# Expert weights turned one at a time and 64-row keys in a block of two expert layers around an attention

## The chip, the cores and the metric

The kernel runs on one core of one Trainium2 chip. The metric is the device time of one execution in microseconds, lower is better. The engines are named as the profile names them: PE (matrix), PEld (its weight loads), DVE (vector), ACT (scalar), POOL (GpSimd), SP (the queue that issues most transfers).

## What is computed

The reference, cut to what matters. The input is 16 sequences of 256 tokens with 128 features, 4096 tokens in all.

```python
x = x + 0.5 * ffn(layernorm(x))      # expert layer 0
x = x + attention(layernorm(x))
x = x + 0.5 * ffn(layernorm(x))      # expert layer 1

def ffn(x):                           # 8 experts, each takes its own 512 best tokens
    scores = softmax(xf @ gate_w.T)
    vals, idx = top_k(scores.T, 512)
    y = layernorm(xf[idx]) * ln_w + ln_b
    h = gelu(y @ fc1s[e].T + b1s[e])              # 128 -> 512
    out = (h @ fc2s[e].T + b2s[e]) * vals         # 512 -> 128
    return xf.at[idx].add(out)

def attention(x):                     # 16 heads of 8 features, causal, 256 tokens
    scores = (q @ k.T + q . pek[distance]) / sqrt(8)
    p = softmax(where(causal, scores, -inf))
    return (p @ v + p . pev[distance]) @ Wo.T
```

## The kernel before, in words

Each engine has its own program, and semaphores set the order between them. There are three parts: `expert_layer(0)`, `attention()`, `expert_layer(1)`.

**Expert layer.** DVE normalises the tokens and finds each expert's 512 tokens with a search of 30 steps. Then the token numbers of the experts come out one expert after another. POOL fetches the tokens: `gather(e)` issues four indirect transfers (L543). It issues the gathers of `AHEAD = 5` experts first, then `scatter(0)`: four indirect transfers that add the results into the output in memory (L554). `scatter(e)` waits until the results of expert e are scaled (`s_os`) and until all transfers of `scatter(e - 1)` have landed (`s_sc`), since both may add to the same row. After each scatter comes the gather of expert e + 5, as long as there is one. In layer 0 the later scatters have two memsets each behind them (L570, L571), which clear a quarter of the key buffer of the attention.

PE turns all weights first: 16 banks of four transposes (L913) through two PSUM banks, which ACT copies out (L700, L702). Then, expert by expert: `turn_rows(e)` turns the fetched tokens (L920), DVE scales them into `yT` (`rows_in`, L1308), `first_half(e)` multiplies with fc1 (L929), ACT takes the gelu (L710), and `second_half(e)` multiplies with fc2 (L939). DVE adds the bias and scales (`scale`, L1293, L1296). PE's order is `first_half(e)`, `turn_rows(e + 1)`, `second_half(e - 1)`, so the first result comes after two first halves. ACT also writes `parity` rows for the attention after each expert of layer 0 (L718).

**Projections.** `attention()` projects queries and keys in 16 pieces (L973). Each piece is split into three bf16 parts whose sum is the fp32 value: `first_part` (ACT, L726), `rest_of` (DVE, L1334), `second_part` (ACT, L730), `third_part` (POOL, L591, and L594 for the odd queries). SP stores each piece to memory (L440). From the fifth piece on, one of the nine loads of the first pair of sequences follows each store (L447). `stacked` lists these loads: six products of query and key parts, times 8 features, make 48 rows of a stack in SBUF; the queries have a second 48 rows. The runs hold 3, 2 and 1 products. A query load of a run repeats one part (a broadcast over the run), so its outermost count is the run's length. `first_part(i)` waits for the store of piece i - 4. PE waits for all nine loads before the first scores.

**Scores.** Eight pairs of sequences with 12 slots each. In a slot, `scores` has two halves u. A half is 16 matmuls with the relative keys (L1002, 128 rows) and 16 with the stacked keys (L1005, 128 rows, of which rows 48 and up hold zeros). Between the halves PE turns the maxima that DVE found in the slot before (`turn_maxima`, L1017). After both halves comes `subtract_maxima` of slot s - 2 (L1025), then a `chunk` of the outputs (L1056 or L1066; the first pair has none before its ninth slot). ACT takes the exponential of slot s - 2 (L778) when the subtraction is done. There are three score buffers of two banks, so `scores(s + 1)` waits for the exponential of slot s - 2. On DVE a slot is `partial_maxima` (L1366, L1368) and `rows_of_maxima` (L1382 to L1385), and in four of 12 slots `reduce_relative` (L1395, L1400).

## Time and profile before

| | us or share |
|---|---|
| median of 3 runs (967.27 to 972.53) | 968.02 |
| the profiled execution | 967.66 |
| its span | 965.9 |
| PE busy | 636.5 |
| DVE busy | 504.7 |
| ACT busy | 297.2 |
| POOL busy | 235.6 |
| share of the chain that ended last: PE | 38% |
| DVE, POOL, ACT | 15%, 14%, 9% |
| SP's queue and DMA | 6% and 5% |

Between the span and the execution's time lie 1.76 us. The stretches of the span: expert layer 0 up to about 228 us, the projections up to about 312 us, the scores up to about 712 us, the output projection and expert layer 1 to the end. A row of a timeline gives start, duration, engine, line, operation, what it writes and reads, the count of merged instructions, and in brackets how long the engine was idle before and what ended that. Starts of PE rows can be subtracted from each other; the durations overlap, since matmuls are pipelined.

### The profile page before, as it was taken

Reading aid. Unit: us, or ns where it says so; the run is one execution under the profiler, and the core shown is the slowest. Engines: PE = TensorE matmul, PEld = TensorE weight load, DVE = VectorE, ACT = ScalarE, POOL = GpSimd, SP = SyncE. Lnnn points to the kernel's source line nnn. Section 1 sums busy time; section 2 is a strip of 40 time slices with the busy share of each in tenths; the row PEclk is TensorE's granted clock in tenths of the full one; section 3 lists DMA queues with packets and bytes.
Section 4 is the critical chain, followed back from the end, with each engine's and each line's share of the span. In section 5 each row is a group of like instructions: output and inputs, shape, how many; then the busy total and the mean of one; then the engine's idle time right before and its main releaser. Section 6 shows DMA issues by size and latency. Waiting matters only on the chain.

```text
span 965.9 us, 29195 instructions
## 1 busy us (share of the span) xinstructions
PE 636.5 (66%) x12366; PEld 516.7 (53%) x12366; DVE 504.7 (52%) x1712; ACT 297.2 (31%) x473; POOL 235.6 (24%) x227
## 2 busy tenths in 40 slices
PE   4512998700733789888898879899972811689640
PEld 3501556500422678777787768788862800357430
DVE  7977222123721567565666557667766777512120
ACT  2390454300522232323232313232332264063210
POOL 2000738884533000000000000014110000346864
PEclk9999999955885599999898979999985555599985
DMA  4272213325355332323222323234342506112322
GB/s 122 59 218 80 53 17 43 34 24 142 132 160 173 92 62 70 59 69 60 69 44 74 52 70 56 65 72 97 75 110 46 175 1 178 24 35 31 45 25 22
DMA packets 99163, 73.27 MB, mean 76 GB/s; under 512 B 26569, under 2 KB 92258, under 8 KB 98914
## 3 DMA queue, kind: packets, MB, share of 16 engines
q1 hardware_dynamic: 85858, 57.01, 23.4%
q0 software_dynamic: 13184, 14.43, 9.2%
q8 instruction: 102, 1.67, 0.8%
q14 instruction: 19, 0.16, 0.1%
HBM read 44.34 MB, written 27.01 MB: 74 GB/s over the span
## 4 chain that ended last, share of the span: by engine, by line
PE 38%; DVE 15%; POOL 14%; issue 11%; ACT 9%; SPq 6%; DMA 5%; DVEq 0%; ACTq 0%; POOLq 0%
PE banks L1002 10%; ACT arena L778 8%; PE banks L1005 7%; POOL x_mid L554 5%; PE banks L1025 5%; POOL out_dram L554 5%; SPq L469 3%; DVE arena L1119 3%; PE banks L1066 2%; PE banks L849 2%; POOL arena L543 2%; PE banks L929 2%; PE banks L913 1%; DMA out_dram<-arena 1%; SPq L440 1%
## 5 line engine op out<-in xcount | busy, mean ns | idle before, releaser
L778 ACT ACTIVATE arena<-banks 128x1024 f32<-128x1024 f32 x96 | 98.3, 1024 | 263.4 <-PE banks L1025 263.4
L1002 PE MATMUL banks<-arena 128*128 128x32 bf16 x3072 | 126.8, 194 | 42.8 <-issue 16.1
L1002 PEld LDWEIGHTS banks<-arena 128*128 128x128 bf16 x3072 | 112.4, 101 | 68.1 <-ACT arena L778 38.7
L1366 DVE TRANSPOSE_TENSOR_REDUCE arena<-banks 128x32 f32<-128x1024 f32 x96 | 120.0, 1250 | 18.1 <-PE banks L1005 13.8
L1005 PE MATMUL banks<-arena 128*128 128x32 bf16 x3072 | 108.6, 178 | 8.6 <-issue 8.6
L1005 PEld LDWEIGHTS banks<-arena 128*128 128x128 bf16 x3072 | 93.6, 97 | 11.3 <-issue 11.3
L543 POOL DMA_INDIRECT arena<-table,arena x64 | 61.5, 961 | 126.2 <-DVE arena L1276 107.7
L607 POOL COPY arena<-arena 128x576 f32 (+1 forms) x8 | 5.3, 668 | 329.6 <-PE banks L1056 329.6
L1382 DVE TENSOR_REDUCE arena<-banks 32x8 f32<-32x64 f32 (+1 forms) x96 | 20.1, 209 | 107.9 <-PE banks L1017 107.8
L710 ACT ACTIVATE arena<-banks,arena 128x512 f32<-128x512 f32 x64 | 44.0, 687 | 85.2 <-PE banks L929 85.2
L1025 PE MATMUL banks<-arena 128*128 128x64 bf16 x1536 | 64.4, 198 | 0.7 <-issue 0.7
L929 PE MATMUL banks<-arena 128*128 128x512 f32 x128 | 61.0, 609 | 3.6 <-DVE arena L1308 3.6
L939 PE MATMUL banks<-arena 128*128 128x128 f32 x512 | 61.8, 281 | 1.6 <-ACT arena L710 1.6
L939 PEld LDWEIGHTS banks<-arena 128*128 128x128 f32 x512 | 60.6, 198 | 3.2 <-ACT arena L710 3.2
L554 POOL DMA_INDIRECT out_dram<-arena x32 | 50.2, 1568 | 33.6 <-DVE arena L1296 15.1
L871 PE MATMUL banks<-arena 128*128 128x1 bf16 x60 | 11.2, 186 | 71.4 <-DVE arena L1228 71.4
L1066 PE MATMUL banks<-arena 128*32 128x128 f32 x1536 | 56.4, 288 | 1.4 <-issue 1.2
L554 POOL DMA_INDIRECT x_mid<-arena x32 | 50.2, 1570 | 24.2 <-DVE arena L1296 14.8
L1025 PEld LDWEIGHTS banks<-arena 128*128 128x128 bf16 x1536 | 54.5, 101 | 1.0 <-issue 1.0
L1056 PE MATMUL banks<-arena 128*9 128x128 f32 x1536 | 52.4, 278 | 3.5 <-ACT arena L785 1.9
L1293 DVE TENSOR_TENSOR arena<-banks,arena 128x512 f32<-128x512 f32 x16 | 11.1, 692 | 82.0 <-DMA x_mid<-arena 33.6
L1308 DVE TENSOR_SCALAR arena<-banks,arena 128x512 f32<-128x512 f32 x16 | 13.0, 810 | 73.1 <-PE banks L920 73.1
(182 smaller groups left out, 1021.4 us busy)
## 6 DMA issues: line engine op xcount, KB each, us to landing
query_parts<-arena SPq DMA_DIRECT2D x8, 768.0 KB, 6.4
arena<-query_parts SPq DMA_DIRECT2D x16, 384.0 KB
table<-arena SPq DMA_DIRECT2D x2, 2176.0 KB, 9.4
arena<-in_L_ffn_fc2s_dram SPq DMA_DIRECT2D x4, 1024.0 KB, 10.8
arena<-query_parts SPq DMA_DIRECT2D x16, 256.0 KB
key_parts<-arena SPq DMA_DIRECT2D x8, 384.0 KB, 7.0
arena<-key_parts SPq DMA_DIRECT2D x8, 384.0 KB
head_outputs<-arena SPq DMA_DIRECT2D x128, 18.0 KB
```

The source lines that it names most:

```text
L543: pool.indirect_dma_start(out=rows[:, s, :], out_offset=None, in_=table[n], in_offset=bass.IndirectOffsetOnAxis(ap=idx[:, s:s + 1], axis=0 ...
L554: pool.indirect_dma_start(out=total[n], out_offset=bass.IndirectOffsetOnAxis(ap=idx[:, s:s + 1], axis=0), in_=osb[:, e % 2, j, :], in_offs ...
L710: nc.scalar.activation(hT[:, e % 2, c, :], psum[:, H_B[k % 2], :], ACT.Gelu_apprx_tanh, bias=b1T[:, e * NC + c:e * NC + c + 1]).then_inc(s ...
L778: nc.scalar.activation(dst, psum[:, 2 * r:2 * r + 2, :].rearrange("p u (h n) -> p u h n", h=H), ACT.Exp, scale=HD ** -0.5).then_inc(s_prob, 1)
L929: pe.matmul(psum[:, H_B[k % 2], :], w1T[:, e, P * c:P * c + P], yT[:, e % 2, :], start=True, stop=True).then_inc(s_h, 1)
L939: last = pe.matmul(o, hT[:, e % 2, c, P * j:P * j + P], w2T[:, e, c, :], start=(c == 0), stop=(c == NC - 1))
L1002: pe.matmul(sc[:, :, 2 * a:2 * a + 2], rel_k[:, y:y + P], q_st[:, r, :, q0 + 2 * a:q0 + 2 * a + 2], start=(a == 0), stop=False, skip_group ...
L1005: last = pe.matmul(sc[:, h], k_st[:, r, h, L * b + P * kb:L * b + P * kb + P], q_st[:, r, h, q0:q0 + 32], start=False, stop=False, skip_gr ...
L1025: last = pe.matmul(psum[:, 2 * (s % 3) + u, 64 * g:64 * g + 64], m_wts[:, s % 3, col:col + 1].to_broadcast([P, P]), eye2, start=False, sto ...
L1056: end = pe.matmul(psum[32 * j:32 * j + HD + 1, bank, P * u:P * u + P], v_pair[:, buffer, 2 * batch + kb, 4 * u + j, :], probs[:, blk, H * ...
L1066: end = pe.matmul(psum[32 * j:32 * j + 32, bank, P * u:P * u + P], rel_v[:, HD * x:HD * x + 32], probs[:, blk, :, q0:q0 + 4], start=(kb == ...
L1366: step(v.tensor_reduce(mp, psum[:, 2 * (s % 3):2 * (s % 3) + 2, :].rearrange("p u (h n) -> p (u h) n", n=32), AX.X, ALU.max, apply_transpo ...
```

## The change

Five things change.

- PE turns the weights of expert 0 only before the first tokens, and those of expert e + 1 between `first_half(e)` and `turn_rows(e + 1)`. `second_half(e)` now follows in the same round. ACT and DVE follow that order. The banks of the transposes are shared in a cycle of three (two for weights, one for tokens) and have exact waits. The parity copies come after all experts.
- POOL issues four gathers ahead instead of five, and its eight memsets are gone. DVE clears rows 32 to 63 of the key buffer with one memset at the start of its attention part.
- The keys' matmuls read rows 0 to 63 only, of keys and of queries.
- `subtract_maxima(s - 2)` comes between the two halves of `scores(s)`, behind `turn_maxima`.
- The six products are listed in another order, and the key parts are stored the other way round, so that a query load of a run reads neighbouring parts instead of repeating one. Where `spread` is true, which is the case for the first pair only, the part and the feature are merged into one outermost dimension of 24, 16 or 8.

```diff
@@ stacked @@
-        Q_PART = (0, 0, 0, 1, 1, 2)
-        K_PART = (0, 1, 2, 0, 1, 0)
+        Q_PART = (0, 1, 2, 0, 1, 0)
+        K_PART = (2, 1, 0, 1, 0, 0)
-        def stacked(pr, r):
+        def stacked(pr, r, spread):
-                    q = qs[c, Q_PART[a], 0:HD, :, bass.ds(pr * PT, PT)]
-                    q = q.unsqueeze(0).to_broadcast([b - a, HD, H, PT])
-                    k = ks[0:b - a, :, :, bass.ds(pr * PT, PT)].rearrange("w d h n -> (w d) h n")
+                    q = qs[c, 0:b - a, :, :, bass.ds(pr * PT, PT)]
+                    k = ks[3 - (b - a):3, :, :, bass.ds(pr * PT, PT)].rearrange("w d h n -> (w d) h n")
+                    if spread:
+                        q = q.rearrange("w d h n -> (w d) h n")
@@ SP: attention @@
-                loads = list(stacked(0, 0))
+                loads = list(stacked(0, 0, True))
...
-                        for dst, src in stacked(pr + 1, 1 - r):
+                        for dst, src in stacked(pr + 1, 1 - r, False):
@@ POOL: expert_layer @@
-                AHEAD = 5
+                AHEAD = 4
...
-                    elif n == 0 and e < E - 1:
-
-                        q, i = 2 * H // 4, e - (E - AHEAD)
-                        pool.memset(k_words[32:64, q * i:q * i + q], 0.0).then_inc(s_zero, 1)
-                        pool.memset(k_words[64:P, q * i:q * i + q], 0.0).then_inc(s_zero, 1)
-                        pool.wait_ge(s_zero, 2 * i + 2)
@@ ACT: expert_layer @@
-                for k in range(NWB):
-                    act.wait_ge(s_tr, tr + NXB + k + 1)
...
+                def weights(e):
+                    k = tr + NXB + 3 * e
+                    act.wait_ge(s_tr, k + 1)
+                    nc.scalar.copy(w1T[:, e, :], tr_bank(k)).then_inc(s_trf, 1)
+                    act.wait_ge(s_tr, k + 2)
+                    nc.scalar.copy(w2T[:, e, :, :],
+                                   tr_bank(k + 1).rearrange("p (c d) -> p c d", c=NC)).then_inc(s_trf, 1)
+
+                weights(0)
                 for e in range(E):
...
+                    if e + 1 < E:
+                        weights(e + 1)
@@ PE: expert_layer @@
+                def turn_weights(e):
+                    for w in range(2):
+                        if w and e:
+                            pe.wait_ge(s_yT, n * E + e)
+                        else:
+                            pe.wait_ge(s_trf, weights_read(n, 2 * e))
+                        bank = tr_bank(tr + NXB + 3 * e + w)
...
                 def turn_rows(e):
                     pe.wait_ge(s_rows[e], 64 * (n + 1))
-                    bank = bank_of(NWB + NXB + e)
+                    pe.wait_ge(s_trf, weights_read(n, 2 * e + 1))
+                    bank = tr_bank(tr + NXB + 3 * e + 2)
...
+                turn_weights(0)
                 turn_rows(0)
                 for e in range(E):
                     first_half(e)
                     if e + 1 < E:
+                        turn_weights(e + 1)
                         turn_rows(e + 1)
-
-                    if 0 < e < E - 1:
-                        second_half(e - 1)
-                    if e >= E - 2:
-                        second_half(e)
+                    second_half(e)
@@ PE: scores @@
-                            last = pe.matmul(sc[:, h], k_st[:, r, h, L * b + P * kb:L * b + P * kb + P],
-                                             q_st[:, r, h, q0:q0 + 32],
+                            last = pe.matmul(sc[:, h], k_st[0:64, r, h, L * b + P * kb:L * b + P * kb + P],
+                                             q_st[0:64, r, h, q0:q0 + 32],
                                              start=False, stop=False, skip_group_check=True)
                         if u == 0 and turn:
                             turn_maxima(s - 1, pr)
+                        if u == 0 and between:
+                            subtract_maxima(s - 2, pr)
@@ DVE @@
-                for e in range(1, E + 1):
-                    if e < E:
-                        rows_in(e)
-                    if e >= 2:
-                        scale(e - 2)
-                scale(E - 1)
+                for e in range(E):
+                    if e + 1 < E:
+                        rows_in(e + 1)
+                    scale(e)
 
             def attention():
 
+                dve.wait_ge(s_tab, 16)
+                v.memset(k_words[32:64], 0.0).then_inc(s_zero, 1)
```

## Rows read from the trace of the kernel before

**Rows 1.** Timeline of POOL in expert layer 0: start, us, engine, line, operation.
```profile
136.24 1.64 POOL L554 DMA_INDIRECT x_mid<-arena  x1 [14.83 <-DVE arena L1296]
...
218.72 1.56 POOL L554 DMA_INDIRECT x_mid<-arena  x1 [0.28 <-POOL arena L571]
```

**Rows 2.** Timeline of POOL in expert layer 1.
```profile
873.37 1.63 POOL L554 DMA_INDIRECT out_dram<-arena  x1 [15.11 <-DVE arena L1296]
...
911.23 1.63 POOL L554 DMA_INDIRECT out_dram<-arena  x1 [0.30 <-issue]
...
950.14 1.55 POOL L554 DMA_INDIRECT out_dram<-arena  x1 [2.74 <-DMA out_dram<-arena]
```

**Rows 3.** Timeline of PE in expert layer 0, from the first weights on.
```profile
107.49 3.35 PE L913 MATMUL banks<-arena 128*128 128x128 f32 x16
...
119.14 0.63 PE L920 MATMUL banks<-arena 128*128 128x128 f32 x4 [0.28 <-ACT arena L700]
120.67 3.89 PE L929 MATMUL banks<-arena 128*128 128x512 f32 x8 [0.90 <-DVE arena L1308]
...
130.06 3.74 PE L939 MATMUL banks<-arena 128*128 128x128 f32 x32
133.64 3.79 PE L929 MATMUL banks<-arena 128*128 128x512 f32 x8
137.26 0.60 PE L920 MATMUL banks<-arena 128*128 128x128 f32 x4
```

**Rows 4.** Timeline of ACT in expert layer 0: a weight copy, a gelu.
```profile
108.64 0.58 ACT L700 COPY arena<-banks 128x512 f32<-128x512 f32 x1 [37.73 <-PE banks L913]
...
137.46 0.69 ACT L710 ACTIVATE arena<-banks,arena 128x512 f32<-128x512 f32 x1 [0.17 <-PE banks L929]
```

**Rows 5.** Timeline of DVE behind expert layer 0.
```profile
231.86 1.64 DVE L1119 BATCH_NORM_STATS2 arena<-arena 128x6 f32<-128x128 f32 x8 [23.19 <-DMA arena<-x_mid]
```

**Rows 6.** Timeline of SP in the projections: two stores, as issued; start, us.
```profile
272.96 5.65 SPq L440 DMA_DIRECT2D key_parts<-arena  x1
...
290.77 6.19 SPq L440 DMA_DIRECT2D query_parts<-arena  x1
```

**Rows 7.** The chain in order of time, its piece before the first scores.
```profile
303.12 8.67 DMA arena<-query_parts
```

**Rows 8.** DMA queues from 262 to 312 us: packets, MB, share of 16 engines.
```profile
q1 hardware_dynamic: 8275, 8.25, 55.3%
```

**Rows 9.** Timeline of PE in the first pair, subtraction and next scores.
```profile
324.86 1.01 PE L1025 MATMUL banks<-arena 128*128 128x64 bf16 x16
326.99 0.67 PE L1002 MATMUL banks<-arena 128*128 128x32 bf16 x16 [1.11 <-ACT arena L778]
```

**Rows 10.** Timeline of PE in one slot of a later pair.
```profile
577.73 0.56 PE L1005 MATMUL banks<-arena 128*128 128x32 bf16 x16
578.14 0.27 PE L1017 MATMUL banks<-arena 128*32 128x128 f32 x1
578.25 0.65 PE L1002 MATMUL banks<-arena 128*128 128x32 bf16 x16
...
579.14 0.63 PE L1025 MATMUL banks<-arena 128*128 128x64 bf16 x16
579.70 1.08 PE L1066 MATMUL banks<-arena 128*32 128x128 f32 x32
580.88 0.66 PE L1002 MATMUL banks<-arena 128*128 128x32 bf16 x16
```

**Rows 11.** Timeline of ACT in the same slot: the exponential.
```profile
579.80 1.02 ACT L778 ACTIVATE arena<-banks 128x1024 f32<-128x1024 f32 x1 [2.62 <-PE banks L1025]
```

**Rows 12.** Timeline of PE in layer 0: 128-row and 32-row matmuls in turn.
```profile
94.21 0.19 PE L895 MATMUL banks<-arena 128*128 128x1 bf16 x1
94.33 0.21 PE L897 MATMUL banks<-arena 32*128 32x1 bf16 x2
94.47 0.19 PE L895 MATMUL banks<-arena 128*128 128x1 bf16 x1
```

More of the change, by code:

```diff
@@ L369, in tr_bank, with weights_read @@
             return psum[:, TR[k % 2], :]
+        def weights_read(n, k):
+            return 2 + n * (NAB + NXB) + NXB + k
         def part_of(i, w):
             if i % 2:
-                return k_part[:, i // 2 % 2, w, :]
+                return k_part[:, i // 2 % 2, 2 - w, :]
             return q_part[:, i // 2 % 2, 512 * w:512 * w + 512]
@@ L444, in attention @@
                             sp.wait_ge(s_pst[b], 16)
-                        sp.wait_ge(s_zero, 8)
+                        sp.wait_ge(s_zero, 1)
                     if i >= 4 and loads:
@@ L695, in expert_layer @@
                 last.then_inc(s_init, 1)
-                for k in range(NWB):
-                    act.wait_ge(s_tr, tr + NXB + k + 1)
-                    if k % 2 == 0:
-                        nc.scalar.copy(w1T[:, k // 2, :], tr_bank(tr + NXB + k)).then_inc(s_trf, 1)
-                    else:
-                        nc.scalar.copy(w2T[:, k // 2, :, :],
-                                       tr_bank(tr + NXB + k).rearrange("p (c d) -> p c d", c=NC)).then_inc(s_trf, 1)
+                def weights(e):
[6 more added lines that the diff above has]
+                weights(0)
                 for e in range(E):
@@ L711, in expert_layer @@
                                              bias=b1T[:, e * NC + c:e * NC + c + 1]).then_inc(s_g, 1)
-                    if n == 0:
-                        if e == 0:
-                            act.wait_ge(s_tr, tr + NAB)
-                            act.wait_ge(s_tab, 16)
-                            act.wait_ge(s_const, 9)
+                    if e + 1 < E:
+                        weights(e + 1)
+                if n == 0:
+                    act.wait_ge(s_tab, 16)
+                    act.wait_ge(s_const, 9)
+                    for e in range(E):
                         nc.scalar.copy(q_words[96:P, 4 * e:4 * e + 4],
@@ L837, in bank_of @@
                 def bank_of(k):
-                    read = 2 + n * (NAB + NXB) + k - 1
-                    if k < NAB + 2:
-                        pe.wait_ge(s_trf, read)
+                    pe.wait_ge(s_trf, 2 + n * (NAB + NXB) + k - 1)
                     return tr_bank(tr + k)
@@ L908, in expert_layer @@
                 pe.wait_ge(s_raw, 64 * (n + 1))
-                for k in range(NWB):
-                    bank, e = bank_of(NXB + k), k // 2
-                    for c in range(NC):
-                        src = raw2[:, e, P * c:P * c + P] if k % 2 else raw1[:, e, c, :]
-                        last = pe.transpose(bank[:, P * c:P * c + P], src, ident)
-                    last.then_inc(s_tr, 1)
+                def turn_weights(e):
[5 more added lines that the diff above has]
+                        bank = tr_bank(tr + NXB + 3 * e + w)
+                        for c in range(NC):
+                            src = raw2[:, e, P * c:P * c + P] if w else raw1[:, e, c, :]
+                            last = pe.transpose(bank[:, P * c:P * c + P], src, ident)
+                        last.then_inc(s_tr, 1)
                 def turn_rows(e):
                     pe.wait_ge(s_rows[e], 64 * (n + 1))
-                    bank = bank_of(NWB + NXB + e)
+                    pe.wait_ge(s_trf, weights_read(n, 2 * e + 1))
+                    bank = tr_bank(tr + NXB + 3 * e + 2)
                     for j in range(NJ):
@@ L986, in attention, with scores @@
                 pe.wait_ge(s_rv, 16)
-                pe.wait_ge(s_zero, 8)
+                pe.wait_ge(s_zero, 1)
                 pe.wait_ge(s_parity, E)
                 pe.wait_ge(s_eye, 1)
-                def scores(s, pr, r, turn):
+                def scores(s, pr, r, turn, between):
                     b, q, later = SLOTS[s]
@@ L1078, in pair @@
                     for s in range(NS):
-                        scores(s, pr, r, turn=s >= 1 or not first)
-                        if s >= 2 or not first:
-                            subtract_maxima(s - 2, pr)
+                        scores(s, pr, r, turn=s >= 1 or not first, between=s >= 2 or not first)
                         if s >= 8 or not first:
@@ L1300, in rows_in @@
                 def rows_in(e):
-                    k = NWB + NXB + e
+                    k = NXB + 3 * e + 2
                     dve.wait_ge(s_tr, tr + k + 1)
@@ L1310, in expert_layer @@
                 rows_in(0)
-                for e in range(1, E + 1):
-                    if e < E:
-                        rows_in(e)
-                    if e >= 2:
-                        scale(e - 2)
-                scale(E - 1)
+                for e in range(E):
+                    if e + 1 < E:
+                        rows_in(e + 1)
+                    scale(e)
             def attention():
+                dve.wait_ge(s_tab, 16)
+                v.memset(k_words[32:64], 0.0).then_inc(s_zero, 1)
                 dve.wait_ge(s_const, 7)
```

## The prediction

> **What bounds the kernel now.** I read the chain of work that ended last first, in order of time, then the timeline of each engine where the chain changes hands. There are four different limits.
>
> In both expert layers the last part is POOL's. POOL had finished its early gathers 14.83 us before it could start its first scatter in layer 0, and 15.11 us in layer 1 [rows 1, 2]. From there on it is never free for long: the eighth scatter starts 82.48 us after the first in layer 0 (218.72 less 136.24) and 76.77 us after it in layer 1. So what counts in an expert layer is when the first scatter can start, and how fast POOL drains. What keeps POOL waiting is PE: it turns all weights from 107.49 to 119.14 before it looks at the first tokens, and then does two first halves before the first second half [rows 3].
>
> The projections end when the last load of the first pair lands: 8.67 us of transfer end the chain there, at 311.8 us [rows 7]. Before that SP stands in the issue of single stores for 5.65 and 6.19 us [rows 6], while the 16 DMA engines together are only 55.3% busy from 262 to 312 us [rows 8]. A queue that is full while the engines are half idle has its work on a few of them.
>
> In the scores a slot closes through ACT. The subtraction starts at 579.14, the exponential runs from 579.80 for 1.02 us, and the next scores start at 580.88, 0.06 us after its end [rows 10, 11]. PE's own chunk ends at 580.78. So this loop and PE's own work are nearly the same length.
>
> **Weights, layer order, gathers.** In layer 0 eight transposes come first instead of 64. The first 16 took 3.35 us [rows 3], so eight end at about 109.2, and ACT's first copy, 108.64 plus 0.58 [rows 4], ends then too. `turn_rows(0)` starts near 109.3 instead of 119.14. From there to the first half it was 1.53 us; I take 1.8, since a transpose took 0.21 us at 107.49 and 0.15 us at 137.26. `first_half(0)` starts at 111.1 instead of 120.67: 9.6 us earlier. From there to `second_half(0)` it was 9.39 us with two first halves. Now one first half takes 3.62 us (133.64 to 137.26), then `turn_rows(1)` waits for ACT: the fourth gelu ends 4.51 us after the half's start (137.46 plus 0.69, less 133.64) [rows 3, 4], a copy of 0.58 and handshakes make it 5.2, four transposes 5.7. I add 1.3 us for a first half on a slow clock, which makes 7.0, a gain of 2.4. Together 12.0 us: the first scatter moves from 136.2 to 124.2. POOL's 16 gathers, four fewer, end before that (it was free at 121.4 with 20). The same steps hold for layer 1.
>
> The drain then has four gathers between scatters instead of three. A scatter with a gather behind it takes 12.62 us (911.23 less 873.37, by 3), one without 9.73 (950.14 less 911.23, by 4) [rows 2]. Four and three make 79.7 us: 3.0 longer than layer 1 had, 2.8 shorter than layer 0 had, whose memsets go. PE's new round, about 5.7 plus 3.58 us, is 9.3 us against POOL's 12.62, so the weights inside the loop are covered; if the clock halved there, a round would pass 12.62 and this cover would be gone. Sum: layer 0 gains 12.0 + 2.8 = 14.8, layer 1 gains 9.0. Together -23.8; I allow -16 to -26.
>
> The memset on DVE and ACT's parity copies cost nothing: DVE is idle for 23.19 us there [rows 5].
>
> **The first pair's loads.** A broadcast query load of three products has an outermost count of 3, one of two products a count of 2. Four such loads move 384 or 256 rows of 1 KB; if each goes to as many engines as its outermost count, that is 128 rows each time on the same two engines. The change makes the counts 24 and 16. Then only the mean load matters: 55.3% of 50 us is 27.7 us [rows 8]. Engines that are evenly loaded need until 290 with that; the computing alone would end earlier. The scores start at about 290.5 instead of 311.9: -21 us. Bounds: 0, if the rows were spread before, and -26, if the stage falls to the pace of its first pieces. I take -21, since two blocked stores of 6 us against half-idle engines are hard to read otherwise.
>
> The Trainium skill has this as a rule (DMA: Bandwidth & Descriptors, section on why a DMA increments its semaphore by 16): the number of engines is the largest up to 16 that divides the slowest dimension of both sides, and a leading broadcast confines a transfer. By it the loads go from 3 and 2 engines to 12 and 16. The trace agrees as far as the blocked queue shows; no row names an engine.
>
> **Subtraction between the halves.** In a pair without chunks PE waited 1.11 us for ACT in each slot [rows 9], 324.86 to 326.99 from subtraction to next scores. With the subtraction half a slot earlier the exponential overlaps the second half. Five slots then give back most of it, I take 0.9 us each: -4.5. What is late next there is the turn of the maxima, behind DVE. In the other 88 slots the gate of ACT goes. It is worth 0.10 us (580.78 to 580.88) by PE's modelled end, up to 0.25 if the end is modelled late; I take 0.2: -17.6. The wait for the turned maxima gets 0.56 us less slack, since the subtraction (579.14 to 579.70) no longer stands before it; chunk and first half stay as its cover.
>
> **64-row keys.** The number of matmuls and their columns stay. But PE now changes between 128-row and 64-row form three more times per slot: into the keys in both halves, and out of them to L1017. No row has 64 rows. The nearest has 32: from L895 with 128 rows to L897 with 32 it takes 0.12 us, and from the second L897 back about as long, where a step in one form takes 0.025 to 0.05 [rows 12]. That is 0.09 us for each change. The other end is L1005 to L1017, from 128 to 32 columns: 16 matmuls from 577.73 to 578.14, so no gap at all, and L1017 to L1002 0.11 us with a 128-column matmul in it [rows 10]. That other end makes it 0. Upwards, a change can hardly cost more than a whole matmul: L1017 lasts 0.27 us [rows 10]. I take 0.09, because L897 changes rows, as the keys do, and L1017 changes columns: 0.27 us per slot, times 96 less a few covered, is +24. Bounds 0 and +78 (0.27 times three times 96).
>
> A rule of the Trainium skill speaks against this part (TensorEngine Tiling (Array Packing), Key Properties): changing the tiling mode drains the engine. L897 agrees, L1017 shows none.
>
> **Sum.** 967.7 - 23.8 - 21 - 4.5 - 17.6 + 24 = 924.8. That is against the profiled execution, 0.4 below the median. I forecast 925.
>
> **Rivals.** The parts are nearly independent, so each rival changes one term.
>
> (a) *The change of form is free*, as at L1017. The +24 goes: 901. PE would then drop to DVE's pace in slots with `reduce_relative`, which may give back some.
>
> (b) *The loads were not confined*, and the queue was full for another reason. The -21 goes: 946. The half-idle engines speak against it.
>
> (c) *Each change costs a whole matmul*, 0.27 us, with the slot bound by PE: +78 instead of +24, so 979, slower than before. It ends on the other side from about 0.25 us a change upwards. Nothing but the size speaks against it: L897 shows a third of that.
>
> (d) *Weight loads no longer hide in the 64-row form.* The two L897 are 0.05 us apart, a step of L1005 is 0.025. For 3072 matmuls that is +77: 1002. Against it: those two stand right behind a change of form.
>
> (e) *PE's round decides the expert layers*, with a slow clock and the copies of weights in it. If half of the 23.8 goes: 937.
>
> **How the numbers follow.** Forecast (910 to 940, with e): 0.62. (a): 0.14. (b): 0.10. (c): 0.06. (d): 0.05. Something not seen: 0.03. The range leaves out the far halves of (a), (c) and (d): 902 to 952. Faster by over 0.5%: 0.91; within 0.5%, about what a measurement can tell from no change: 0.02; slower: 0.07. The likeliest case's own range is 910 to 940.
>
> **What would show it.** Right: the first scatter starts about 12 us earlier in both layers, later ones 12.6 and then 9.7 us apart; SP's stores are issued in under 2 us each, and the scores start about 72 us after the last scatter of layer 0 starts, instead of 93; the next scores no longer start 0.06 us after an exponential; L1005 starts 0.1 us or more behind the last L1002. Wrong: a step of the keys above 0.03 us; PE waiting for `s_T` in each slot; POOL waiting for DVE between scatters; stores that still block.

## The result: slower, 1000.4 us

The changed kernel takes 1000.42 us (median of 4 runs, 995.38 to 1004.24) against 970.08 us (967.27 to 972.53) for the kernel before in runs on the same chip: ratio 1.031, interval 1.025 to 1.037. The forecast was 925. The kernel before was run anew with each group of experiments: 971.5 us beside e1 to e4, 965.2 beside e5 to e8, 970.9 beside e9 to e12, 965.0 beside e13 to e15. So kernels of different groups are compared by their ratios below, where 0.01 is 9.7 us; the ratios leave out the few runs in a slower state that the kernels have, one each of e1_first_only, e2_before_merged and e9_paced_128. The profiled execution took 995.38 us, with a span of 993.6 us. In the changed kernel lines are shifted: L554 is now L558, L1002 is L1006, L1005 is L1009, L1025 is L1031, L1017 is L1023, L469 (the loads of later pairs) is L473.

**What came as forecast.** The timeline of POOL, changed kernel, layer 0 (first scatter, second, sixth) and layer 1, to be held against [rows 1, 2]:

```profile
123.19 1.63 POOL L558 DMA_INDIRECT x_mid<-arena  x1 [6.84 <-DVE arena L1300]
...
135.80 1.62 POOL L558 DMA_INDIRECT x_mid<-arena  x1 [0.30 <-issue]
...
183.44 1.55 POOL L558 DMA_INDIRECT x_mid<-arena  x1 [2.42 <-DMA x_mid<-arena]
...
898.05 1.64 POOL L558 DMA_INDIRECT out_dram<-arena  x1 [7.11 <-DVE arena L1300]
```

The first scatter starts at 123.19 instead of 136.24; 124.2 was forecast. The next comes 12.61 us later, those without a gather behind them 9.7 us apart. POOL waits half as long as before (6.84 and 7.11 us, instead of 14.83 and 15.11).

The projections: the timeline of SP and then the chain in order of time, changed kernel, against [rows 6, 7]:

```profile
265.69 1.27 SPq L444 DMA_DIRECT2D key_parts<-arena  x1
...
271.15 0.38 SPq L444 DMA_DIRECT2D query_parts<-arena  x1
```
```profile
271.57 6.00 DMA arena<-query_parts
...
277.71 0.65 PE banks L1006 x16
```

No store blocks any more, and the scores start at 277.71. In the kernel before they start at 311.9: 34 us, of which the expert layer brings 16 (its last scatter starts at 202.80 instead of 218.72).

A slot of the scores, timeline of PE, changed kernel, against [rows 10]:

```profile
543.12 0.66 PE L1006 MATMUL banks<-arena 128*128 128x32 bf16 x16
543.71 0.56 PE L1009 MATMUL banks<-arena 64*128 64x32 bf16 x16
544.20 0.28 PE L1023 MATMUL banks<-arena 128*32 128x128 f32 x1
544.32 0.63 PE L1031 MATMUL banks<-arena 128*128 128x64 bf16 x16
544.79 0.66 PE L1006 MATMUL banks<-arena 128*128 128x32 bf16 x16
545.38 0.56 PE L1009 MATMUL banks<-arena 64*128 64x32 bf16 x16
545.87 1.08 PE L1072 MATMUL banks<-arena 128*32 128x128 f32 x32
546.88 0.66 PE L1006 MATMUL banks<-arena 128*128 128x32 bf16 x16
```

A slot is 3.76 us, before it was 3.65. L1006 to L1009 is 0.59 us where 128-row keys take 0.49 (the median of the kernel before), and L1009 to L1023 is 0.49 instead of 0.41: 0.10 and 0.08 for a change of form, where 0.09 was taken. Right here the kernel is 0.11 us per slot slower, and the forecast had 0.07 (0.27 less 0.2).

**Where the time went.** All of this leaves the changed kernel 34 us ahead when the scores start. From the first to the last start of the scores it then needs 462 us, the kernel before 390. The waits of PE in the scores (in all, how often, the longest), changed kernel:

```profile
PE banks L1009 <- issue: 37.3, 6, 8.4
PE banks L1006 <- issue: 33.6, 7, 6.4
PE banks L1031 <- issue: 10.7, 1, 10.7
```

and before, with the gate of ACT under it:

```profile
PE banks L1002 <- issue: 16.1, 6, 3.6
PE banks L1002 <- ACT arena L778: 10.6, 19, 2.5
PE banks L1005 <- issue: 8.6, 5, 3.1
```

"issue" is a wait for nothing that the profile shows. It is 82 us in all, 27 before. These are not many short waits but 14 holes of over 2 us, 82 us together (before: eight, 24 us). One of them, timeline of PE and then of SP, changed kernel:

```profile
339.17 0.28 PE L1023 MATMUL banks<-arena 128*32 128x128 f32 x1
339.29 0.19 PE L1031 MATMUL banks<-arena 128*128 128x64 bf16 x1
350.17 0.96 PE L1031 MATMUL banks<-arena 128*128 128x64 bf16 x15 [10.69 <-issue]
```
```profile
329.82 0.85 SPq L473 DMA_DIRECT2D arena<-query_parts  x1
330.78 0.79 SPq L473 DMA_DIRECT2D arena<-key_parts  x1
331.76 1.50 SPq L473 DMA_DIRECT2D arena<-query_parts  x2
...
337.10 3.05 SPq L473 DMA_DIRECT2D arena<-query_parts  x1
```

PE breaks off in the middle of 16 matmuls of one line, after the first. No semaphore stands there. SP has just put out all nine loads of the next pair in 10 us. In the kernel before, the same loads took SP 28 us, and two of them together held it for 9.44 us (timeline of SP):

```profile
358.95 9.44 SPq L469 DMA_DIRECT2D arena<-query_parts  x2
```

The queues of the DMA engines (packets, MB, share of 16 engines), changed kernel from 333 to 347 us, then before from 357 to 384 us:

```profile
q1 hardware_dynamic: 1432, 1.41, 98.3%
q8 instruction: 1, 0.02, 0.9%
```
```profile
q1 hardware_dynamic: 1864, 1.87, 26.7%
q8 instruction: 6, 0.10, 1.9%
```

So the loads of the later pairs changed too, although the diff leaves them their three dimensions. The new source, `qs[c, 0:b - a]`, steps from product to product by 8 features and from feature to feature by one, so both steps are multiples of one row length, the two dimensions are one, and it comes out with an outermost count of 24 or 16, with or without the `rearrange`. The flag `spread` does nothing. That is worked out from the shapes; that the fold is what matters is shown below, by one row of padding (e1_first_only). Before, the broadcast (a step of zero) could not fold. The Trainium skill's rule (DMA: Bandwidth & Descriptors, section on why a DMA increments its semaphore by 16) takes the count from the slowest dimension as the instruction carries it. The 98.3% against 26.7% agree with it.

And q8 carries instructions: 88 packets of 16 KB in the scores of either kernel, one about every 4 us, on the same engines. Around the hole above, one of them starts at 331.22 us and the next only at 346.26. It takes 2.01 us, and PE goes on 1.90 us after its end. The queues from 332 to 346 us, where q8 has no packet, and from 346 to 347 us:

```profile
q1 hardware_dynamic: 1554, 1.53, 98.6%
```
```profile
q8 instruction: 1, 0.02, 12.6%
```

### The profile page after: what moved, and what is told of

Its sections match the earlier page's. It is cut to its first block, busy times and chain, and to the rows that moved or that the text cites. A ratio compares the mean times of both kernels' runs of the same rounds, so it can differ in the third digit from the quotient of the medians.

```text
span 993.6 us, 29188 instructions
## 1 busy us (share of the span) xinstructions
PE 664.2 (67%) x12366; PEld 540.8 (54%) x12366; DVE 510.0 (51%) x1713; ACT 294.7 (30%) x473; POOL 221.4 (22%) x219
## 4 chain that ended last, share of the span: by engine, by line
PE 48%; issue 16%; DVE 15%; POOL 13%; DMA 5%; ACT 1%; SPq 1%; DVEq 0%; POOLq 0%; ACTq 0%
PE banks L1006 10%; PE banks L1009 9%; PE banks L1072 6%; PE banks L1031 5%; PE banks L1062 5%; POOL out_dram L558 5%; POOL x_mid L558 4%; DVE arena L1123 3%; POOL arena L547 2%; PE banks L1023 2%; PE banks L848 2%; DMA x_mid<-arena 1%; DVE arena L1370 1%; PE banks L870 1%; PE banks L883 1%
## 5 line engine op out<-in xcount | busy, mean ns | idle before, releaser
L1006 PE MATMUL banks<-arena 128*128 128x32 bf16 x3072 | 127.4, 194 | 38.6 <-issue 33.6
L1006 PEld LDWEIGHTS banks<-arena 128*128 128x128 bf16 x3072 | 107.1, 102 | 60.0 <-issue 57.5
L1009 PE MATMUL banks<-arena 64*128 64x32 bf16 x3072 | 110.7, 176 | 37.3 <-issue 37.3
L1009 PEld LDWEIGHTS banks<-arena 64*128 64x128 bf16 x3072 | 90.8, 95 | 47.4 <-issue 37.9
L1031 PE MATMUL banks<-arena 128*128 128x64 bf16 x1536 | 69.0, 203 | 10.7 <-issue 10.7
L1031 PEld LDWEIGHTS banks<-arena 128*128 128x128 bf16 x1536 | 67.0, 106 | 13.0 <-issue 11.0
L1072 PE MATMUL banks<-arena 128*32 128x128 f32 x1536 | 60.1, 305 | 0.3 <-issue 0.3
L558 POOL DMA_INDIRECT out_dram<-arena x32 | 50.3, 1571 | 23.4 <-issue 8.5
L558 POOL DMA_INDIRECT x_mid<-arena x32 | 50.2, 1568 | 22.9 <-issue 8.5
L870 PEld LDWEIGHTS banks<-arena 128*128 128x128 bf16 x60 | 6.3, 104 | 76.9 <-DVE arena L1232 76.9
L1072 PEld LDWEIGHTS banks<-arena 128*32 128x32 f32 x1536 | 45.4, 122 | 3.3 <-issue 0.9
## 6 DMA issues: line engine op xcount, KB each, us to landing
arena<-in_L_ffn_fc2s_dram SPq DMA_DIRECT2D x4, 1024.0 KB, 10.7
```

The costliest lines, as they stand in the source:

```text
L558: pool.indirect_dma_start(out=total[n], out_offset=bass.IndirectOffsetOnAxis(ap=idx[:, s:s + 1], axis=0), in_=osb[:, e % 2, j, :], in_offs ...
L1006: pe.matmul(sc[:, :, 2 * a:2 * a + 2], rel_k[:, y:y + P], q_st[:, r, :, q0 + 2 * a:q0 + 2 * a + 2], start=(a == 0), stop=False, skip_group ...
L1009: last = pe.matmul(sc[:, h], k_st[0:64, r, h, L * b + P * kb:L * b + P * kb + P], q_st[0:64, r, h, q0:q0 + 32], start=False, stop=False, s ...
L1031: last = pe.matmul(psum[:, 2 * (s % 3) + u, 64 * g:64 * g + 64], m_wts[:, s % 3, col:col + 1].to_broadcast([P, P]), eye2, start=False, sto ...
L1072: end = pe.matmul(psum[32 * j:32 * j + 32, bank, P * u:P * u + P], rel_v[:, HD * x:HD * x + 32], probs[:, blk, :, q0:q0 + 4], start=(kb == ...
```

## The experiments

The first theory: the merged loads of pairs 1 to 7 fill all 16 engines, and PE's instructions come late behind them. The rivals: PE's own new program (64 rows, the place of the subtraction) makes the holes; or the writes into SBUF do.

| kernel | us | ratio to before, interval | scores, first to last start | slot, median | PE's "issue" waits |
|---|---|---|---|---|---|
| before | 970.1 | | 390 | 3.65 | 26.6 |
| changed | 1000.4 | 1.031 (1.025 to 1.037) | 462 | 3.76 | 81.9 |
| e1_first_only | 935.1 | 0.963 (0.953 to 0.972) | 393 | 3.76 | 18.5 |
| e2_before_merged | 1008.9 | 1.035 (1.028 to 1.042) | 456 | 3.65 | 89.0 |
| e3_before_first_only | 950.8 | 0.981 (0.973 to 0.990) | 390 | 3.65 | 24.2 |
| e4_first_only_128 | 916.4 | 0.944 (0.937 to 0.952) | 381 | 3.47 | 24.3 |
| e5_paced | 916.6 | 0.950 (0.944 to 0.956) | 383 | 3.76 | 15.5 |
| e6_before_64 | 992.6 | 1.026 (1.020 to 1.033) | 419 | 4.05 | 20.8 |
| e7_before_between | 959.0 | 0.993 (0.990 to 0.996) | 378 | 3.47 | 19.4 |
| e8_ffn_only | 940.5 | 0.974 (0.968 to 0.980) | 388 | 3.65 | 26.1 |
| e9_paced_128 | 912.3 | 0.939 (0.934 to 0.944) | 373 | 3.47 | 31.3 |
| e10_pitch | 997.7 | 1.028 (1.022 to 1.034) | 466 | 3.76 | 82.6 |
| e11_threes | 967.5 | 0.999 (0.995 to 1.002) | 429 | 3.76 | 46.3 |
| e12_paced_128_behind | 920.4 | 0.949 (0.946 to 0.953) | 383 | 3.65 | 23.4 |
| e13_dram_burst | 967.8 | 1.002 (0.999 to 1.005) | 433 | 3.76 | 51.6 |
| e14_later_128 | 904.0 | 0.938 (0.934 to 0.942) | 364 | 3.47 | 22.3 |
| e15_later_64 | 917.5 | 0.951 (0.947 to 0.955) | 382 | 3.76 | 13.4 |

The first column is the median of all runs. The last three columns are from the one profiled execution of each kernel; the slot is the median distance of one slot's start to the next.

### Is it the loads or PE's program?

e1_first_only, against the changed kernel:

```diff
+        qs_later = nc.dram_tensor("query_parts_later", [2, 3, HD + 1, H, TOK], BF16).ap()
...
-                    q = qs[c, 0:b - a, :, :, bass.ds(pr * PT, PT)]
+                    q = (qs if spread else qs_later)[c, 0:b - a, 0:HD, :, bass.ds(pr * PT, PT)]
```

and the stores of pairs 1 to 7 go to `qs_later`.

> The changed kernel with only the first pair's loads merged: the parts of the later pairs lie in a DRAM tensor with a pad behind each product, so that product and feature do not fold into one row of equal steps. Theory 1 (the merged loads of pairs 1 to 7 come as bursts over all 16 DMA engines and TensorE's instruction fetch waits behind them): TensorE's idle that nothing shows falls from 82 us to about 25, the scores stage from 474 us to about 405, the time to about 930. Theory 2 (the stalls come from TensorE's own new program, its 64-row form and the place of the subtraction): the stalls of 5 to 11 us stay, the time stays near 1000.

e2_before_merged is the kernel before with the diff's new `Q_PART`, `K_PART`, `part_of` and `stacked` and nothing else:

> The kernel before with the new order of the parts and the new load lines alone, which come out merged for every pair. Theory 1: the projections end some 20 us earlier, and the scores stage gains stalls of 5 to 10 us worth about 57 us and a lower clock after them: about 1005. Theory 2: about 949, the 20 us of the projections and nothing else.

e3_before_first_only is e2_before_merged with the `qs_later` of e1_first_only:

> The kernel before with the loads as the change describes them: merged for the first pair, not for the others (padded DRAM tensor). Both theories: the term of the forecast alone, 970 less 18 to 21, about 950. If the time is above 960, the gain of the first pair is lost elsewhere.

One row of padding between the products takes 65 us off the changed kernel (1000.4 to 935.1) and 58 off e2_before_merged (1008.9 to 950.8; by the ratios it is 52). The new load lines alone, in a kernel whose PE program is the old one, bring the holes. The timeline of PE in e2_before_merged, where L1003 is the old L1002:

```profile
359.38 0.28 PE L1003 MATMUL banks<-arena 128*128 128x32 bf16 x4
370.59 0.53 PE L1003 MATMUL banks<-arena 128*128 128x32 bf16 x12 [10.93 <-issue]
```

Of the 69 us between the scores of the changed kernel and of e1_first_only (462 less 393), 63 are "issue" waits (81.9 less 18.5). Most of the rest is PE's clock. The share granted over the scores is 0.84 in the changed kernel and 0.92 in e1_first_only; it is 1.00 from 318.8 to 339.4 us, before the hole shown above, and 0.50, the lower of two levels, from 350.2 to 356.0 behind it. Without all idle time the slots add up to 373 us against 364. PE's new program is ruled out as the cause of the holes.

### How long the queue is

e5_paced, against the changed kernel, with the loads merged as they are:

```diff
-                        for dst, src in stacked(pr + 1, 1 - r, False):
-                            sp.dma_start(dst, src).then_inc(s_load[1 - r], 16)
+                    def load(slots):
+                        for i in slots:
+                            if loads:
+                                if i:
+                                    sp.wait_ge(s_score, NS * pr + i)
+                                sp.dma_start(*loads.pop(0)).then_inc(s_load[1 - r], 16)
+                    load(range(0, 2))
...
+                    load(range(2, 6))
...
+                    load(range(6, 9))
...
```

The stores of the outputs stand between the three groups of loads.

> The changed kernel with its merged loads as they are, but SyncE puts one load of the next pair behind each slot of the scores (a wait for the slot's score semaphore before loads 2 to 9, the stores of outputs in between). Theory 1a, the stalls need a queue of several loads on all 16 engines at once: they go, and the time is that of e1_first_only, 930 to 940. Theory 1b, each merged load alone (384 rows of 1 KB at about 130 ns over 16 engines, 3 us) holds the fetch back: nine short stalls per pair of up to 1 to 2 us stay, 950 to 975. If the loads are not the cause at all: 1000.

e11_threes is the same with three loads behind each of the slots 0, 3 and 6:

> The changed kernel with its merged loads in three groups of three, behind slots 0, 3 and 6. A dose between all nine at once (1000) and one at a time (917). If a stall is as long as the queue ahead of a fetch, three short stalls of about 2 to 3 us per pair: 935 to 960. If a burst of any size costs a stall of 5 to 10 us: 1000 or more.

All at once 1000, three at a time 967.5, one at a time 916.6: the holes of over 2 us sum up to 82, 41 and 12 us, the longest are 10.7, 6.5 and 3.4 us. What costs is how much is queued at once, not how many engines a load uses; theory 1a holds and 1b falls. e5_paced even comes out ahead of e1_first_only, by 12 us by the ratios (0.950 against 0.963, with intervals that just overlap). This was not expected, and e7_before_between shows a cause (below). e11_threes lies 7 us above the range that I gave it.

### Engines or SBUF?

e13_dram_burst, against e5_paced:

```diff
+                    if not last:
+                        for j, (dst, src) in enumerate(stacked(pr + 1, 1 - r, False)):
+                            n = dst.shape[0]
+                            sp.dma_start(spare[r, j, 0:n], src).then_inc(s_spare, 16)
```

> e5_paced (917) with nine additional transfers at the start of each pair but the last, the same merged rows as the pair's loads, but from DRAM to DRAM and all at once. They write nothing into SBUF and nobody waits for them. If the stalls come from the occupied DMA engines, on which TensorE's instruction fetch must run too, they are back: 980 to 1010, holes of 5 to 10 us in TensorE's matmuls, no 16 KB fetch in them. If they come from the writes into SBUF, the time stays below 930.

50 us more than e5_paced by the ratios, brought on by transfers that touch no SBUF and that nobody waits for. But they do not act alone. The timeline of PE, that of SP, and the queues from 303 to 311 us:

```profile
303.52 0.28 PE L1027 MATMUL banks<-arena 64*128 64x32 bf16 x4
310.60 0.50 PE L1027 MATMUL banks<-arena 64*128 64x32 bf16 x12 [6.79 <-issue]
```
```profile
294.90 0.85 SPq L480 DMA_DIRECT2D arena<-query_parts  x1
...
300.47 11.36 SPq L480 DMA_DIRECT2D arena<-query_parts  x2
```
```profile
q1 hardware_dynamic: 754, 0.74, 100.1%
q8 instruction: 1, 0.02, 1.7%
```

The last of the nine transfers to DRAM landed at 300.8 us, 3 us before this hole began. What fills the engines in the hole are the pair's own loads into SBUF: they stood in SP's queue behind the burst, and six of them went out together from 294.90 to 302.4 us. In the later pairs too, most holes of over 2 us begin about when the burst has landed, with two to four such loads behind it. So these holes do not tell DRAM from SBUF.

What transfers to DRAM do by themselves stands earlier in the bursts. In the fifth pair the burst goes out from 505.50 us on and the first load into SBUF at 512.56. The instruction packets start at 503.6 and 511.2 us, 7.6 us apart where 4.3 is the median, and PE stands still (its timeline):

```profile
511.66 0.41 PE L1024 MATMUL banks<-arena 128*128 128x32 bf16 x8
513.45 0.41 PE L1024 MATMUL banks<-arena 128*128 128x32 bf16 x8 [1.38 <-issue]
```

Where PE's loop turns, e5_paced has a second hole of 2.6 and 2.9 us; here it is 4.9 and 5.8 us, and those two began with only the burst in flight. Occupied engines are enough to hold the instructions up, without a write into SBUF. That they are enough for all of the 50 us is not shown.

The effect is below the 980 to 1010 that I expected. A 1 KB row took 46 ns at the median in the bursts to DRAM against about 125 ns in the bursts of the changed kernel, so the same number of rows kept the engines busy for less time; this fits, but nothing tests it.

e10_pitch asks where those 125 ns come from:

```diff
-        qs = nc.dram_tensor("query_parts", [2, 3, HD, H, TOK], BF16).ap()
-        ks = nc.dram_tensor("key_parts", [3, HD, H, TOK], BF16).ap()
+        qs = nc.dram_tensor("query_parts", [2, 3, HD, H, TOK + 64], BF16).ap()
+        ks = nc.dram_tensor("key_parts", [3, HD, H, TOK + 64], BF16).ap()
```

> The changed kernel with its merged bursts, the rows of the two DRAM tensors 64 elements longer, so that the rows of one load no longer lie at a distance of 8192 bytes. Theory P (the reads of a burst are slow, 132 ns for 1 KB instead of 46, because of this distance): packets back near 50 to 60 ns, bursts of 4 to 5 us instead of 15, stalls of PE a third: about 960. Theory N (it is the number of engines at work, whatever the distance): packets stay at 130 ns, time stays at 1000.

Nothing changes: 121 ns at the median, 82.6 us of "issue". A distance of 8320 bytes instead of 8192 does not help. Larger distances were not tried, so why the rows take that long stays open.

### The terms one by one

e8_ffn_only is the changed kernel with loads, scores and 128-row keys as before the change:

> The kernel before with the expert layers alone as in the change (weights turned one expert at a time, 4 gathers ahead, the memset on VectorE, here for rows 32 to 127). My term: minus 23.8, so 946. If what POOL gains is given back in the projections behind it: 955 or more.

940.5, ratio 0.974: 25 us, forecast 23.8.

e6_before_64:

```diff
-                            last = pe.matmul(sc[:, h], k_st[:, r, h, L * b + P * kb:L * b + P * kb + P],
-                                             q_st[:, r, h, q0:q0 + 32],
+                            last = pe.matmul(sc[:, h], k_st[0:64, r, h, L * b + P * kb:L * b + P * kb + P],
+                                             q_st[0:64, r, h, q0:q0 + 32],
```

> The kernel before with the keys' matmuls on 64 rows and nothing else. My term: three changes of form in each slot at 0.09 us, plus 24 us, so 995. The pair e1_first_only and e4_first_only_128 (935 and 916) says 19 us, so 990. If the gate of ScalarE hides it here: 970 to 975. If the 64-row form costs a whole matmul each time: above 1030.

Ratio 1.026, 25 us, forecast 24. That the two agree is in part luck: the slot grows by 0.40 us, not by 0.27, since here, with the subtraction behind both halves, a fourth change of form (keys to subtraction) lies in it. In 88 slots that would be 35 us, of which 25 arrive; PE's "issue" waits are 6 us shorter than before. The timeline of PE, where keys to turned maxima is 0.52 us and turned maxima to the next half 0.12:

```profile
587.44 0.59 PE L1005 MATMUL banks<-arena 64*128 64x32 bf16 x16
587.96 0.28 PE L1017 MATMUL banks<-arena 128*32 128x128 f32 x1
588.08 0.65 PE L1002 MATMUL banks<-arena 128*128 128x32 bf16 x16
```

e4_first_only_128 is e1_first_only with 128-row keys:

> The same as e1_first_only, with the keys' matmuls on all 128 rows again and rows 64 to 127 of the keys cleared on VectorE. If the changes of form cost what the slot shows (0.28 us, 96 slots), it is 25 to 27 us faster than e1_first_only, near 903. If the 64-row form is free beyond the slot or hidden, within 5 us of e1_first_only. If the 64-row form was what made the stalls, it is 60 us or more faster than the changed kernel where e1_first_only is not.

It takes 916.4 us, 19 less than e1_first_only (18 by the ratios) where 25 to 27 were expected. The slot is 0.29 us shorter, 25 us in 88 slots. New waits stand against it: 7.3 us in all for ACT's copies of the outputs (L788) and 3.1 us for the loads of the second pair.

e7_before_between puts the subtraction between the halves:

```diff
                         if u == 0 and turn:
                             turn_maxima(s - 1, pr)
+                        if u == 0 and between:
+                            subtract_maxima(s - 2, pr)
```

> The kernel before with the subtraction between the halves and nothing else. My terms: minus 17.6 for the gate of ScalarE (0.2 us in 88 slots) and minus 4.5 in the first pair: 948. If VectorE's turned maxima become the gate instead: 960 to 970.

This term was mis-sized: 6 us (959.0 against 965.2 in its runs), forecast 22. The slot is 0.18 us shorter where 0.2 was taken. The waits of PE in e7_before_between, where L1058 is the chunk:

```profile
PE banks L1058 <- ACT arena L785: 11.5, 3, 5.4
PE banks L1002 <- DMA arena<-query_parts: 4.9, 1, 4.9
...
PE banks L1002 <- ACT arena L778: 2.7, 6, 1.6
```

The gate of the exponential falls from 10.6 to 2.7 us, and two others stand there. The chunk waits for ACT L785, which copies the last output. And the second pair waits 4.9 us for its loads, at 358.14 us: the first pair, 5.8 us shorter but for that, now ends before they have landed. Both together cost 14.5 us more than before, and 22 less 14.5 leaves 7.5, near the 6 measured. Timelines of PE, of ACT and of SP at the longest wait for L785:

```profile
443.21 1.89 PE L1058 MATMUL banks<-arena 128*9 128x128 f32 x32 [5.36 <-ACT arena L785]
```
```profile
442.57 0.58 ACT L785 COPY arena<-banks 128x512 f32<-128x512 f32 x1 [8.01 <-DMA head_outputs<-arena]
```
```profile
405.87 9.92 SPq L469 DMA_DIRECT2D arena<-query_parts  x2
415.89 5.56 SPq L469 DMA_DIRECT2D arena<-key_parts  x1
421.63 8.37 SPq L469 DMA_DIRECT2D arena<-query_parts  x2
...
433.15 3.67 SPq L453 DMA_DIRECT2D head_outputs<-arena  x4
```

ACT needs its buffer stored, the store stands in SP's queue behind nine loads, and these are slow because each runs on few engines: from 403.28, when the first load went out, to 433.15. In the kernel before PE waited for L785 only 1.9 us. So the confined loads have a price of their own, which shows as soon as the slot is shorter. It is in e1_first_only (3.4 us of waits for the copy) and e4_first_only_128 too. It is one reason why paced loads beat confined ones: with one load per slot the stores go out between them, and PE never waits for the copy in e5_paced. That covers 3.4 of the 10 us between the scores of the two kernels, and "issue" another 3; the rest stays open.

e9_paced_128 and e12_paced_128_behind take this out:

> The paced loads of e5_paced together with the keys on 128 rows: 916.6 less 25.4 (what e6_before_64 shows for the 64-row form) is 891. If a slot falls to the pace of VectorE instead, about 900. If the 64-row form costs only 19 us here too, as between e1_first_only and e4_first_only_128, 898.

> As e9_paced_128, with the subtraction behind both halves, as before the change: what the move is worth where SyncE's queue holds nothing up. My term says 22 us slower than e9_paced_128 (0.2 us in 88 slots and 4.5 in the first pair). e7_before_between, where the confined loads hold up the stores, says 7.

With the stores free, the move of the subtraction is worth 8 us (920.4 to 912.3; by the ratios 10), still not 22, though near the 7 that e7_before_between gave. 128-row keys are worth 11 us by the ratios (0.950 to 0.939, give or take 8), not 19 to 25: the expectation for e9_paced_128 missed. The slots are as they should be, 3.47 us against 3.65 and 3.76. What eats the gain is "issue" once more: 31.3 us in e9_paced_128, 23.4 in e12_paced_128_behind, 15.5 in e5_paced. In 88 slots the move brings 16 us (0.18 each) and "issue" takes 8 of them, which leaves 8 where 8 to 10 were measured. 128-row keys bring 25 us (0.29 each) and "issue" takes 16, which leaves 9 where 11 were measured. A PE that gets through its instructions faster seems to run dry sooner behind the same loads.

e14_later_128 and e15_later_64 put each load one slot later (slots 1 to 9), so none meets the first slot of a pair:

> e9_paced_128 (912) with each load one slot later, behind slots 1 to 9: none in the first slot of a pair, where the loop turns and TensorE's program starts to be fetched anew. If load and turn of the loop compete, some 2 us for each of the three turns and the first pair's stall of 6 us go: 900 to 905. If the turn costs its two holes of 3 us whatever the loads do: 910 to 914.

> The same with the keys on 64 rows, to e5_paced (917) what e14_later_128 is to e9_paced_128. Its slot is 0.29 us longer than that of 128 rows (3.76 against 3.47), which is 25 us over 88 slots; e9_paced_128 and e5_paced differ by 4. If the rest is lost because a faster TensorE stalls more behind the same loads, the gap between e14 and e15 stays 4 to 10; if it was the turn of the loop, it opens to 15 or more.

The two kernels are 13.5 us apart here, in one group of runs. Against e9_paced_128 and e5_paced neither has moved by the ratios (0.938 against 0.939, 0.951 against 0.950), so keeping the loads out of the first slot is worth nothing that these runs can tell, and between the two answers that e15_later_64 was to decide it does not decide. The profiled execution of e14_later_128 has 22.3 us of "issue" where that of e9_paced_128 has 31.3, among them no stall of 6 us in the first pair; with one execution each this is a hint. The two neighbouring holes of 2 to 4 us at each of two turns of the loop are there in both kernels, 12 us in all, whether a load is near or not. Of the 25 us of the slot 13.5 arrived, and "issue" takes 9 (22.3 less 13.4).

**A kernel that beats both.** e14_later_128 takes 904.0 us, 0.938 of the kernel before: the diff's expert layers and the subtraction between the halves, all loads merged, one load per slot, keys on 128 rows. e9_paced_128 is as fast within the intervals.

## Why the prediction was wrong, point by point

**Expert layers, -23.8.** Right: 25 us alone. First scatter at 123.19 where 124.2 was derived, POOL's distances 12.6 and 9.7. Rival (e), PE's round on a slow clock, did not come: from one first half to the next it is 9.3 us (111.32 to 120.59, timeline of PE), below POOL's 12.6.

**The first pair's loads, -21.** Right: e3_before_first_only has ratio 0.981, which is 18 us. Its scores start at 295.5 instead of 311.9. Rival (b) is out.

**64-row keys, +24.** The cost of one change is right, the slot in the changed kernel too: 0.29 us more than with 128 rows, forecast 0.27. The +25 in the kernel before is four changes, partly covered, and not the three of the forecast. Around the changed kernel the term is worth 11 to 18 us (e5 to e9, e15 to e14, e1 to e4). The 0.09 us of [rows 12] for 128 to 32 rows is also the price from 128 to 64 rows, in and out, and L1017, which changes columns only, shows nothing in either kernel. Rivals (a) and (c) are out by the price of a change, 0.08 to 0.10 us where they had 0 and 0.27; rival (d) is out since the steps within a group did not change (0.56 us for 16 matmuls in both forms). The rule of the Trainium skill (TensorEngine Tiling (Array Packing), Key Properties) that a change of tiling mode drains TensorE agrees with 0.09 us at the rows' change and is not visible at the columns' change.

**Subtraction, -17.6 and -4.5.** Mechanism right, size wrong: the slot lost its 0.18 us and the first pair 5.8, the kernel gained 6. I asked what is late next behind the gate only among PE, ACT and DVE, and not in SP's queue. Rows that were there to read: the loads hold SP for 28 us per pair, and the stores that ACT needs stand behind them. These two sizes are misses, but not what turned the sign.

**The step that failed** is a half sentence in the part on the first pair's loads: "The change makes the counts 24 and 16". I applied it to the first pair, as the flag in the diff says, and took the loads of the other seven pairs as unchanged. With the parts in order, product and feature have steps that fold into one, whoever asks for it. The arithmetic for it stands in the diff and the shape `[2, 3, HD, H, TOK]`. None of the rivals had it.

The second half of the failure is that even had I seen it, I would have booked it as a gain or as nothing. In the kernel before no pair behind the first waits for its loads, and the engines are 26.7% busy. Faster loads off the critical path look harmless. They were not: a transfer that finishes early by filling every engine takes them from PE's instructions, 82 us of "issue" waits instead of 27. The forecast for the change as it was described, e1_first_only, would have been 10 us too low (925 against 935.1) and inside the range; the fold cost 65. That nearness has some luck in it: the subtraction gave some 15 us less than forecast, and the 64 rows cost some 6 to 13 less.

## What to carry to other kernels

Work out the access pattern that comes out, not the one that is written: two dimensions with steps that fit each other become one, and transfers that kept the engines 26.7% busy fill all 16. Before speeding up a transfer nobody waits for, look at what else the DMA engines carry, above all the instruction queue of an engine with thousands of small instructions. Then spread the transfers over the time that there is (one per slot was worth about 79 us here, by the ratios), and look in the issuing queue for who stands behind them.

## What the runs showed of the hardware

PE needs its instructions over the same DMA engines as the data. In the scores 16 KB come about every 4 us. With the 16 engines full for 10 to 15 us, PE stood still for 5 to 11 us in the middle of a line's matmuls (the changed kernel, e2_before_merged). What ends a hole is in the traces too: the scores of all 17 have 124 "issue" waits of over 2 us, and every one ends 1.2 to 2.0 us after a 16 KB packet of q8 has ended. A moment taken at random lies that near behind such a packet in about a fifth of the time. In the changed kernel 14 packets start over 6 us after the one before, the latest 15.05 us after it; in the kernel before six do, the latest 8.44 us. So the missing thing is the instructions, and what is late is their packet. When PE asked for it, no trace tells.

The Trainium skill (DMA: Bandwidth & Descriptors, section on queues, rings and completion order) says that an engine takes turns between its queues packet by packet, a packet being typically 9 to 17 descriptors. By an estimate from this and the 0.125 us of a 1 KB row here, a fetch would wait some 1.1 to 2.1 us for its turn. The packet of the hole above came about 11 us later than the usual 4 us after the one before, so a single turn does not explain it.

A row of 1 KB took 46 ns at the median in the projections of the changed kernel (245 to 278 us), where the 16 engines were 91.7% busy and moved 251 GB/s, and about 125 ns in the bursts between the scores (20 us from each burst's first load). Bursts from DRAM to DRAM took 46 ns. Rows 128 bytes further apart do not change it (121 ns in e10_pitch).
